# Recurrent attention block on one core: three of four chunks divided inside the attention, the last product given four input buffers, and the diagonal's odd row sums moved to TensorE in every quad

## The reference, cut to what matters

```python
xn = layernorm(x)                              # x: (2, 2048, 512) f32
q, k, v = xn @ Wq, xn @ Wk, xn @ Wv            # 16 heads of 32
scores = einsum('bthd,bshd->bhts', q, k) * tril   # masked scores are 0, not -inf
attn = softmax(scores / sqrt(2048), axis=-1)
s = einsum('bhts,bshd->bthd', attn, v) @ Wo
g = silu(layernorm(xn)*gamma+beta @ ternary(Wf).T + bias)
out = x + s * g
```

## Time and profile before

| | us |
|---|---|
| median of the runs | 1556.85 |
| the profiled execution, its own time | 1554.97 |
| its span | 1553.2 |
| attention's last product with the values on TensorE, from the span's start | about 1427 |

### The profile page before, as it was taken

How to read it: one execution, slowest core, us unless ns; L and a number is a source line. 1 busy time by engine, 2 the same in 40 slices (tenths; PEclk the granted TensorE clock), 3 DMA queues, 4 the chain that set the end, 5 groups by cost and what they waited for, 6 DMA issues and landing times.

```text
span 1553.2 us, 24547 instructions
## 1 busy us (share of the span) xinstructions
PE 1495.3 (96%) x8554; PEld 904.9 (58%) x8554; DVE 1053.1 (68%) x2389; ACT 774.7 (50%) x1614; POOL 871.1 (56%) x723
## 2 busy tenths in 40 slices
PE   6999999999999999999999999999999999998877
PEld 5888888887444555455454554555555555544655
DVE  7545656643787777777777777777777777752566
ACT  4333322332555666665656666665666665665110
POOL 4100000000666877877778777787777877679341
PEclk9999999999899999999999999999999999999988
DMA  6668866548851442324145145142324511313998
GB/s 209 189 178 229 259 190 177 164 135 232 197 130 36 83 109 63 80 69 113 36 110 130 36 89 123 50 95 68 93 52 92 130 36 39 96 40 86 323 343 277
DMA packets 110426, 201.42 MB, mean 130 GB/s; under 512 B 14688, under 2 KB 32736, under 8 KB 109280
## 3 DMA queue, kind: packets, MB, share of 16 engines
q1 hardware_dynamic: 99216, 177.86, 43.0%
q10 hardware_dynamic: 11088, 22.02, 4.3%
HBM read 123.22 MB, written 76.28 MB: 128 GB/s over the span
## 4 chain that ended last, share of the span: by engine, by line
PE 81%; DVE 6%; DMA 4%; POOL 3%; ACT 3%; issue 1%; SPq 1%; ACTq 0%; POOLq 0%; DVEq 0%
PE psP L1287 21%; PE psS L1365 17%; PE psO L1388 16%; PE psM L1265 16%; PE psL L1394 6%; DMA gr<-gate 3%; DVE psM L1073 2%; POOL acc L814 2%; PE psT L1212 2%; PE psL L1403 2%; DVE mx L1076 1%; ACT Pb L937 1%; ACT acc L937 1%; POOL Pb L797 1%; DVE oo L1200 1%
## 5 line engine op out<-in xcount | busy, mean ns | idle before, releaser
L814 POOL TENSOR_TENSOR acc<-acc,Pb 128x1024 f32<-128x1024 f32 (+2 forms) x308 | 600.2, 1977 | 159.3 <-PE psO L1388 128.6
L937 ACT ACTIVATE Pb<-psS 128x512 f32<-128x512 f32 (+2 forms) x1122 | 518.2, 533 | 296.6 <-PE psS L1365 288.6
L1076 DVE TENSOR_REDUCE mx<-psM 128x1 f32<-128x512 f32 x768 | 484.9, 683 | 158.8 <-PE psM L1265 157.6
L1365 PE MATMUL psS<-half 97*128 97x512 f32 (+1 forms) x1247 | 473.9, 397 | 7.0 <-ACT Pb L937 4.6
L1265 PE MATMUL psM<-half 96*128 96x512 f32 (+3 forms) x1280 | 457.9, 383 | 6.6 <-DVE mx L1073 3.1
L1365 PEld LDWEIGHTS psS<-half 97*128 97x128 f32 x1247 | 234.4, 190 | 245.5 <-issue 105.3
L1265 PEld LDWEIGHTS psM<-half 96*128 96x128 f32 x1280 | 235.7, 190 | 77.1 <-DVE mx L1076 26.3
L1073 DVE CUSTOM_DVE_ANT_0 psM<-psM,negm 128x256 f32<-128x256 f32 (+3 forms) x512 | 238.2, 517 | 62.1 <-PE psM L1265 61.9
L1388 PE MATMUL psO<-Pb,Vs 128*32 128x512 f32 (+3 forms) x2304 | 267.6, 534 | 0.9 <-POOL Pb L797 0.9
L797 POOL TENSOR_SCALAR_AFFINE_SELECT Pb<-Pb 128x256 f32<-128x256 f32 x240 | 93.9, 406 | 81.0 <-ACT Pb L937 78.9
L1394 PE MATMUL psL<-Pb,ones 128*32 128x512 f32 (+3 forms) x1072 | 125.6, 537 | 0.0
(11 more groups left out here) (101 smaller groups left out, 1479.5 us busy)
## 6 DMA issues: line engine op xcount, KB each, us to landing
half<-q_hi SPq DMA_DIRECT2D x32, 512.0 KB, 10.4
half<-k_hi SPq DMA_DIRECT2D x32, 512.0 KB, 10.5
xt<-in_L_attn_x SPq DMA_DIRECT2D x8, 1024.0 KB, 7.9
q_hi<-st_hi SPq DMA_DIRECT2D x32, 256.0 KB, 4.4
q_lo<-st_lo SPq DMA_DIRECT2D x32, 256.0 KB, 4.8
gate<-gs SPq DMA_DIRECT2D x32, 256.0 KB, 2.2
k_hi<-st_hi SPq DMA_DIRECT2D x32, 256.0 KB, 2.8
k_lo<-st_lo SPq DMA_DIRECT2D x32, 256.0 KB, 2.9
```

The lines of the kernel that those rows point to most:

```text
L814: g.tensor_tensor(to[:, :, o:], to[:, :, o:], Pb[s % RING][:, heads, o:], ALU.add).then_inc(sum_done, 1)
L937: a.activation(weights(s, h)[:, o:], score_bank(s * HQ + h, last)[:, o:], ACT.Exp, scale=SCALE).then_inc(exp_done, 1)
L1076: ins = v.tensor_reduce(flat[:, heads, slots], bank[:, 0:ns * w].rearrange("p (a b c) -> p a b c", a=nh, c=w), AX.X, ALU.max)
L1365: t.matmul(score_bank(n, last)[:, o:], Ks[par][j // HALF][0:MROW + 1, h, j % HALF * P:(j % HALF + 1) * P], Qs[par][c // 2][0:MROW + 1, h, ...
```

## The change

Three things at once; in the diff `qn` is the quad, `c` the chunk.

1. `summed(gr)` no longer depends on the quad: TensorE makes the row sums of the odd diagonal steps of chunks 1 to 3 in all eight quads.
2. Chunks 0, 1 and 2 of each quad are divided inside the attention. SP spreads a chunk's 4 rows of denominators over 128 partitions (`divisors`, four transfers), VectorE takes reciprocals of [128, 16] before step 8, 22 or 27 (`RECIPROCALS_AT`), SP writes them to device memory, waits, and reads them back into `E`, each row over 32 partitions (`back`, one and four transfers), GpSimd multiplies `cum` by `E` after the first group of chunk 2, the first and the third of chunk 3 (`DIVIDED_AT`), and SP stores the quotient (`store_divided`). The next use of the same `cum` and `E` comes after that store, so `load_chunk` is later and `masked_keys` moves by two groups (chunks 2, 3) or one (the next quad's chunk 0). In SP's list the next quad's `load_half` (its high half) moves from chunk 1's time to chunk 2's, `load_values` from there to just before chunk 3. Only chunk 3 keeps the old way.
3. The tail: x and gate have four buffers (`NX`), the first pair is loaded in the last quad, all its transfers are SP's, only one chunk of each batch is spread and multiplied, the PSUM banks are rotated by one, and the first chunk's product waits only for the last exponentials, not for the last `psO` and `psL`, the first chunk's high part is taken between two steps of the last quad, the loop over batches is written out, and the last chunk is stored in four parts.

The diff, cut to its core:

```diff
-def summed(gr, last):
+def summed(gr):
     c, j = GROUPS[gr]
-    return not (last and c > 0 and j >= CT * c)
+    return c == 0 or j < CT * c
...
-    found = [(qn, c) for c in range(NCH) if gr == FIRST[c] + (c > 0) and (c or qn == 0)]
-    if gr == FIRST[NCH - 1] + 4 and qn + 1 < NQUAD:
+    found = [(qn, c) for c in range(NCH) if gr == FIRST[c] + (0, 1, 3, 3)[c] and (c or qn == 0)]
+    if gr == FIRST[NCH - 1] + 5 and qn + 1 < NQUAD:
...
+NDIV = NCH - 1
+RECIPROCALS_AT = {STEPS.index((1, 4)): 0, STEPS.index((2, 10)): 1, STEPS.index((3, 3)): 2}
+DIVIDED_AT = {FIRST[2]: 0, FIRST[3]: 1, FIRST[3] + 2: 2}
+NX = 4
...
+            def divisors(qn, c):
+                i = c % 2
+                sp.wait_ge(lst_done, START + qn * NCH + c + 1).then_inc(sp_waited, 1)
+                for h in range(HQ):
+                    sp.dma_start(lc[h * DH:(h + 1) * DH, :], E[i][h * DH:h * DH + 1, :]).then_inc(lc_in, 16)
+
+            def back(qn, c):
+                i, k = c % 2, qn * NDIV + c
+                rows = bass.ds((NCH * qn + c) * HQ, HQ)
+                sp.wait_ge(lc_done, k + 1)
+                sp.dma_start(d_rows[rows, :].rearrange("h (i p) -> (h i) p", p=HQ * CW // P), lc[:]).then_inc(d_out, 16)
+                sp.wait_ge(d_out, (k + 1) * 16)
+                for h in range(HQ):
+                    sp.dma_start(E[i][h * DH:(h + 1) * DH, :],
+                                 d_rows[bass.ds((NCH * qn + c) * HQ + h, 1), :].broadcast_to([DH, CW])).then_inc(d_in[i], 16)
+
+            def store_divided(qn, c):
+                sp.wait_ge(div_done, qn * NDIV + c + 1)
+                sp.dma_start(num_t[bass.ds(qn * P, P), c * CW:(c + 1) * CW], cum[c % 2][:]).then_inc(ost_out[c % 2], 16)
...
             def quad(qn, par, more, follows):
+                if follows:
+                    store_last(qn - 1)
+                    load_chunk(qn, 1)
+                    sp.wait_ge(pv_done, START + qn * NSTEP)
                 if not more:
+                    sp.wait_ge(lst_out, START + NQ * 16)
                     denominators(0)
                     sp.dma_start(wo_s[:], w_o).then_inc(wo_in, 16)
                 if follows:
-                    store_chunk(qn - 1, NCH - 1)
-                    load_chunk(qn, 1)
-                store_chunk(qn, 0)
-                store_maxima(qn, 2)
+                    store_maxima(qn, 2)
+                divisors(qn, 0)
+                back(qn, 0)
+                if not follows:
+                    store_maxima(qn, 2)
+                store_divided(qn, 0)
                 load_chunk(qn, 2)
                 if more:
-                    sp.wait_ge(pv_done, START + qn * NSTEP)
                     load_half(qn + 1, 1 - par, 1)
-                    load_values(qn + 1, 1 - par)
-                if not more:
+                else:
                     ...
+                    load_numerators(0, 0)
+                    load_numerators(0, 1)
-                store_chunk(qn, 1)
+                divisors(qn, 1)
                 store_maxima(qn, 3)
+                back(qn, 1)
+                if more:
+                    load_values(qn + 1, 1 - par)
+                    store_maxima(qn + 1, 0)
+                else:
+                    load_numerators(0, 2)
+                    sp.wait_ge(pv_done, START + qn * NSTEP + STEPS.index((2, 0)))
+                    load_xg(0)
+                divisors(qn, 2)
+                store_divided(qn, 1)
                 load_chunk(qn, 3)
-                if more:
-                    store_maxima(qn + 1, 0)
-                store_chunk(qn, 2)
+                back(qn, 2)
+                store_divided(qn, 2)
                 if more:
                     load_chunk(qn + 1, 0)
                     store_maxima(qn + 1, 1)
                 else:
-                    reciprocals(0)
-                    spread(0, 0)
+                    spread(0)
                     sp.wait_ge(wo_done, 2)
-                    spread(0, 1)
+                    load_numerators(0, NDIV)
...
+            denominators(1)
+            for n in range(1, NX):
+                load_xg(n)
+            def chunk(n, b, c):
+                if n == 1:
+                    spread(1)
+                parts = [slice(j, j + 1) for j in range(CT)] if n + 1 == NCHUNK else [slice(0, CT)]
+                for part in parts:
+                    sp.wait_ge(oo_done, START + n * CT + part.stop)
+                    sp.dma_start(out_v[n][:, part], oo[c % 2][:, part]).then_inc(oo_out[c % 2], 16)
+                if n + NX < NCHUNK:
+                    load_numerators(1, c)
+                    load_xg(n + NX)
...
+                def divide(qn, c):
+                    i = c % 2
+                    pool.wait_ge(ost_done, START + qn * NCH + c + 1)
+                    pool.wait_ge(d_in[i], (qn * (2 - i) + c // 2 + 1) * HQ * 16)
+                    g.tensor_tensor(cum[i][:], cum[i][:], E[i][:], ALU.mult).then_inc(div_done, 1)
...
                     for masked in masked_keys(qn, gr):
                         later_keys(*masked)
+                    if gr in DIVIDED_AT:
+                        divide(qn, DIVIDED_AT[gr])
...
+                    if not more and gr == NG - 4:
+                        high(0, 0, 0)
...
                     for s in (2 * gr, 2 * gr + 1):
+                        if s in RECIPROCALS_AT:
+                            dve.wait_ge(lc_in, (qn * NDIV + RECIPROCALS_AT[s] + 1) * HQ * 16)
+                            v.reciprocal(lc[:], lc[:]).then_inc(lc_done, 1)
                         for h in range(HQ):
                             maxima(max_share(qn, s, h))
```

More of the change, by code:

```diff
@@ L95, in diagonals_before, with summed_before @@
     return sum(on_diagonal(i) for i in range(s))
-def summed(gr, last):
+def summed(gr):
     c, j = GROUPS[gr]
-    return not (last and c > 0 and j >= CT * c)
-def summed_before(gr, last):
-    return sum(summed(g, last) for g in range(gr))
+    return c == 0 or j < CT * c
+def summed_before(gr):
+    return sum(summed(g) for g in range(gr))
+NSUM = summed_before(NG)
 OWN_STEPS = 19
@@ L833, in quad @@
                         select(s + 1)
-                        if j > CT * c and summed(gr, not more):
+                        if j > CT * c and summed(gr):
                             add(gr - 1)
@@ L940, in _, with high @@
             exps(0, 0)
+            def high(n, b, c):
+                act.wait_ge(D_full, START + (n - 1) * CT)
+                for k in values_in(act, b, c):
+                    a.copy(ah[c % 2][:, k, :], ac[c][:, k, :]).then_inc(ah_done, 1)
             def exp_masked(qn, c):
@@ L1174, in quad @@
                 if not more:
+                    low(0, 0, 0)
                     numerators(qn, NCH - 1)
@@ new lines, in chunk @@
+            def chunk(n, b, c):
+                A, L, out_banks = ah[c % 2], al[c % 2], [psD[out_bank(c, j)] for j in range(CT)]
+                pe.wait_ge(exp_done, START + NQUAD * NSTEP * HQ)
+                if n:
+                    pe.wait_ge(ost_done, START + NQUAD * NCH)
+                    pe.wait_ge(lst_done, START + NQUAD * NCH)
+                for j in range(CT):
+                    pe.wait_ge(sg_done, START + (n - 2) * CT + j + 1)
+                    for k in range(KT):
+                        if j == 0:
+                            pe.wait_ge(ah_done, n * KT + k + 1)
+                        for w in (wo_h, wo_l):
+                            t.matmul(out_banks[j][:], A[:, k, j * P:(j + 1) * P], w[:, k, :],
+                                     start=(k == 0 and w is wo_h), stop=False)
+                pe.wait_ge(al_done, START + (n + 1) * KT)
+                for j in range(CT):
+                    for k in range(KT):
+                        ins = t.matmul(out_banks[j][:], L[:, k, j * P:(j + 1) * P], wo_h[:, k, :],
+                                       start=False, stop=(k == KT - 1))
+                    ins.then_inc(D_full, 1)
@@ L1467 @@
+            tail(chunk)
 _INS = ["L0_attn_x", "L0_attn_Wq", "L0_attn_Wk", "L0_attn_Wv", "L0_attn_Wo", "L0_ffn_weight", "L0_ffn_bias",
```

237 lines of the change are left out of this document (95 added, 142 removed).

## The result

The changed kernel takes **1546.99 us** (median of 4 runs, 1545.45 to 1547.72) against 1556.81 us for the kernel before on the same chip: ratio 0.9935, 95% interval 0.9918 to 0.9952, 9.8 us less. On another chip it was 1545.66 against 1555.13, ratio 0.9943 (0.993 to 0.9956). The profiled execution took 1547.01 us with a span of 1545.3. The forecast was 1543.6.

A forecast was written before the change was run, and what follows sets the result against it. The prediction took TensorE to bound the quads and transfers the tail. Its terms, -30.5 + 10.9 + 1.4 + 2.5 + 2.5 = -13.2 us, taken from 1556.85, gave 1543.6 us, range 1534 to 1557.

The forecast's parts named there:

- The bound: Middle quad: TensorE is busy 126.86 of 128.10 us; time given to it is paid unless it falls on a wait.
- Part 1, the tail: Tail: shortened to TensorE's floor, -30.5 us, bounds -25 to -32.
- three pieces: Tail: eight chunks at TensorE's pace -27.3 us, sooner start -1.3, shorter end after the last addition -1.9.
- transfers' price: Tail: the 28.3 MB left take 73 us at 390 GB/s, under TensorE's 88.8, so costed at nothing.
- R1: Rival, tail: transfers still set it, 93 us at 304 GB/s; 5 to 6 us over the forecast, 1549; chance 0.17.
- Part 2, row sums: Row sums on TensorE: six middle quads +10.0 us, first quad +0.9, last 0; sum +10.9 (4.5 to 18).
- R2: Rival, middle quads: row sums mostly fill waits, costing 5 us instead of 10.9; total 1538; chance 0.13.
- Part 3, divisions: Divisions inside the attention: +0.2 us a quad, +1.4 in all, plus +2.5 in the first quad and +2.5 in the last.
- Chunk 1's copies: Middle quad: copies of chunk 1's denominators land at 866, ahead of VectorE's bank at 870.76; room 4 us.
- R3: Rival, quads: reciprocal's copies late on SP's one queue hold VectorE, then TensorE; at 3 us a quad 1565; chance 0.10.
- The first quad's maxima: First quad: chunk 2's maxima, now behind chunk 0's return, go out at 433.8 instead of 431.32; +2.5 us (1 to 4).
- The last quad: Last quad, chunk 3: GpSimd gains two multiplications of 1.28 us, with a partly hidden wait; +2.5 us (1 to 6).

The follow-up runs named there:

- e1: Changed kernel with the odd diagonal row sums of quads 0 to 6 back on GpSimd: 1534.61 us, ratio 0.9863 to the kernel before.
- e3: Kernel before with only the row sums moved to TensorE in every quad: 1569.08 us, ratio 1.009.
- e10: e4 with the second batch's reciprocals spread between the loads of the second and third tile: 1537.04 us, ratio 0.9892 to the kernel before.
- e11: Changed kernel with each batch's spread of the reciprocals made twice: 1556.75 us, ratio 1.0012 to the kernel before.
- e4: Changed kernel with the odd row sums of two more groups of the last quad's chunk 3 on TensorE: 1542.96 us, ratio 0.9917 to the kernel before.
- e9: The changed kernel itself timed once more, unedited, on another chip: 1545.66 us, ratio 0.9943 to the kernel before.
- e2: Changed kernel with only chunk 1's odd row sums on TensorE in quads 0 to 6: 1539.46 us, ratio 0.9906 to the kernel before.
- e7: Changed kernel with VectorE's split of the last product's weights made earlier, in the last quad's chunk 2: 1544.62 us, ratio 0.9934 to the kernel before.
- e6: Changed kernel with the first quad's chunk 2 maxima stored ahead of chunk 0's return again: 1546.69 us, ratio 0.9948 to the kernel before.
- e8: Changed kernel with the edits of e1, e4, e6, e7 and the second batch's spread earlier: 1525.05 us, ratio 0.9811 to the kernel before.
- e12: e8 with the third reciprocals on VectorE one step later: 1521.79 us, ratio 0.9788 to the kernel before.

## Why the prediction was right, and where its terms were not

**The bound (right).** Time given to TensorE inside a quad is paid: e1 gives back 11.2 us, e3 costs 12 to 14. The earlier trace rows could be taken at their word, 126.86 of 128.10 us.

**Part 1, the tail (right, -30.4 for -30.5).** Its three pieces held one by one. TensorE's stretch from the first product to the last low matmuls went from 112.3 to 85.5, for 85.0 foreseen; the start came 1.3 us sooner, as foreseen; the end behind the last low matmuls 2.3, for 1.9. The transfers' price was right too: 390 GB/s was foreseen, and the queue moved 388 to 394 while it was loaded. What the working left out is the time in which it is not loaded. It set 73 us of transfers under TensorE's 88.8 and priced them at nothing; but SP issues nothing from 1475.4 to 1484.55 us, where it waits for the small write, and then only the 64 KB pieces until 1492.04: 16.6 us, as much as the cover. e10 and e11 show that this decides whether TensorE waits, since a wait in SP's list holds all that is behind it. The tail sat at the point where TensorE's floor and SP's list meet; e11 took 10.6 us for 8.6 us of issues and a landing, and e4 lost 5.5 us at the same place, in both cases a good part of it by the clock. R1 named this stand, priced it by bytes, and did not come in; it was closer than the working said. It was also added up wrongly: 3 + 93 us are a tail of 96, against 95.2 in the forecast, and not 5 to 6 us over it. The tail's length could not have told the two apart; TensorE's waits, 1.4 us in it, do.

**Part 2, row sums (right: 11.1 for the six middle quads by e1 where 10.0 were foreseen, 11.2 in the total for 10.9).** Chunk 1 +0.25 exactly, chunks 2 and 3 +0.88 and +0.85 for 0.71: nothing was given back there, the upper end of the bounds. In the first quad the sums cost chunk 1 some 0.9 us by themselves and chunk 2 0.8 (48.03 in e9, 47.19 in e1), where 0 was said of both. R2 is refuted, by e1, e2 and e3. The Trainium skill, Perfetto Trace Analysis, section "Identifying the Most-Contended Engine", judges how much room TensorE has by the share of peak arithmetic and by the busy share of weight loads. By the second TensorE would be half idle. Here weight loads are busy 67.27 of 130.10 us and added matmuls cost full time; the measurement decides against the rule for this mix of small matmuls.

**Part 3, divisions (cost right, margins thin).** The divisions cost 0.2 us a middle quad by e1, as foreseen. The reciprocal took 0.25 us for 0.15. Chunk 1's copies were foreseen at 866 for a bank at 870.76, a room of 4 us; in the changed kernel, whose quad is 7.84 us later, they came at 877.20, so at 869.4 by that count, and the room was about 1. Chunk 2's wait of 1.3 us was foreseen as 0.5 and hidden by the banks of `psM`. R3 was not the case in the changed kernel but is real: it takes 0.5 us of one quad there (54.99 for 54.45 at a wait of 1.96), and in e2 it took 1.7 us itself and 4.6 with the clock that fell behind it.

**The first quad's maxima (2.5 foreseen, 1.1 alone, 0.4 beside the sums).** SP's queue, beside the earlier trace rows:

```profile
429.88 0.35 SPq L705 DMA_DIRECT2D d_rows<-lc  x1
431.32 1.71 SPq L708 DMA_DIRECT2D E<-d_rows  x4
433.08 2.56 SPq L610 DMA_DIRECT2D half<-mrow  x4
```

They went out at 433.08 and not at 433.8, because the write landed 1.4 us after its issue where 2.3 was taken from a read of 64 KB. The other part is slack: a delay of 1.3 us of the maxima, counted from the quad's start, cost 1.1 us alone and 0.4 once the sums delayed the same step.

**The last quad (wrong in size: +6.8 for +2.5, past the upper end of 6).** The failed term is "+2.5 us for the first two with a partly hidden wait". The count, from the two GpSimd timelines: divisions 3.33 + 1.28 = 4.6 us; the wait for `E` 1.0; the two masked multiplications and the iota 3.9 for 3.0, beside VectorE's `al`; additions 29.6 for 31.1 (the 12.46 of the earlier trace rows and 18.69 for the other eight), so 1.6 less. That is +4.9 where 2.6 plus a part of a wait was foreseen. Then TensorE: from the start of the selections to the chunk's end it is 7.34 us after and 5.39 before, +1.95. It had waited 3.22 and 2.22 us for exponentials and selections, and its matmuls ran at half the rate behind that (1.71 us from `psO` to `psL`, 0.88 before): the granted clock between 1440 and 1450 is 0.63, and 1.00 in the last 9 us of that chunk in the kernel before. (There it is 0.83 between 1405 and 1415 us, behind a wait of 2.00 us, but at that point the chunk waits for GpSimd and it costs nothing that shows.) Together 6.85 for the measured 6.8. e4 and e10 confirm the cause: with two groups fewer on GpSimd the waits and the clock's fall are gone, and the chunk takes 40.2 us, less than before.

On the first of these the Trainium skill, SBUF — State Buffer, section "Who interferes with whom", says that a VectorE instruction with two inputs in SBUF and a GpSimd instruction that reads SBUF hold each other off, the later one until the earlier one ends. The trace agrees: `wo_l` ended at 1411.60, the division had begun at 1409.42, and 2.18 + 1.28 = 3.46 us for the 3.33 measured; without the overlap (e7) it took 1.29.

**Sum.** Foreseen -13.2, measured -7.9 in the spans and -9.8 in the medians. The last quad's 4.3 us are most of the gap; every other stage came within 1.2 us of its forecast.

## What to carry to other kernels

When a queue's list holds a wait, count what is issued ahead of it and what stands behind it: the write came back after 6.8 us with 2 MB ahead and 13.1 with 4, and all behind it was late though the DMA engines had room. When two profiles of one place differ, look at the granted clock there before looking for a cause in the edit. When work goes onto an engine that bounds a stage, add to its own duration what its neighbour's instructions do to it and what the waiting TensorE loses in clock. A change that joins several ideas is judged part by part: here the new tail was worth 30 us in its stage and the row sums cost 11.

## What the runs showed that was not expected

- Two independent delays of one step overlap: 0.9 and 1.1 us alone, 1.3 together (e1, e6, e8).
- Eight of TensorE's matmuls of 512 columns took 0.88 us from start to start of the next kind in one kernel and 1.71 in the other at the same place, behind waits of 0.85 us and of 3.22 and 2.22; a wait of TensorE can cost more than its length.
- The same kernel differs by 1.5 us in one chunk (49.51 and 48.03 us) between two profiles, with a granted clock of 0.83 and 1.00 in ten of its microseconds; in e8 it is 0.83 between 1380 and 1390 us, though TensorE's longest wait in the 5 us ahead of it was 0.32 us.
- Slack behind a late copy ends at about 1.4 us of VectorE's wait: 1.3 are free, 2.1 cost 0.7, 3.1 cost 4.6 (once, in e2), of which 1.7 by the wait and the rest by the clock that fell behind it.
- Moving one 0.25 us instruction by one step was worth about 2 us in seven quads and removed a scatter (e12).
